# Routed experts: the second bias added by VectorE in fp32 at the copy out of PSUM, instead of by a product on TensorE

## The reference

```
h      = concat(patch embedding, n-gram text embedding)        # [64, 229, 128]
h      = h + attention(layernorm(h))
t      = layernorm(h)
shared = sum over 2 shared experts of gelu(t W1 + b1) W2 + b2
probs  = softmax(t gate_w + gate_b); the top 2 of 8 experts e per row, weight p
routed = sum over those 2 of p * (gelu(t rW1[e] + rb1[e]) rW2[e] + rb2[e])
out    = h + shared + routed
```

## Time and profile before

| | |
|---|---|
| runs | 1188.53, 1191.96, 1196.56 us |
| median | 1191.96 us |
| profiled execution | 1194.19 us |
| its span in the trace | 1192.5 us |
| granted TensorE clock, mean | 0.99 |
| busy share of the span | PE 96%, PEld 72%, DVE 80%, POOL 71%, ACT 66% |

### The profile page before, as it was taken

How to read it: one execution, slowest core, us unless ns; L and a number is a source line. 1 busy time by engine, 2 the same in 40 slices (tenths; PEclk the granted TensorE clock), 3 DMA queues, 4 the chain that set the end, 5 groups by cost and what they waited for, 6 DMA issues and landing times.

```text
span 1192.5 us, 31733 instructions
## 1 busy us (share of the span) xinstructions
PE 1142.3 (96%) x9318; PEld 860.6 (72%) x9318; DVE 950.8 (80%) x2484; ACT 791.6 (66%) x1835; POOL 842.8 (71%) x808
## 2 busy tenths in 40 slices
PE   7999999999999999889999989999999999999998
PEld 4777777777777778644545468998989999955555
DVE  5788898888888888879976756676767777779997
ACT  2566666666766666546554557777777777768886
POOL 4446877777778786667887857777777777776664
PEclk9999999999999999989999999999999999999999
DMA  7245555555655553433344234454554444449998
GB/s 218 64 138 144 158 149 158 154 159 150 170 156 155 165 141 99 124 102 104 108 114 122 83 63 101 96 94 92 91 95 93 98 95 98 88 89 208 201 199 167
DMA packets 242871, 152.10 MB, mean 128 GB/s; under 512 B 153852, under 2 KB 221561, under 8 KB 242708
## 3 DMA queue, kind: packets, MB, share of 16 engines
q1 hardware_dynamic: 201684, 102.21, 34.7%
q0 software_dynamic: 36992, 40.97, 16.0%
q10 hardware_dynamic: 4032, 6.88, 2.2%
HBM read 70.74 MB, written 56.32 MB: 107 GB/s over the span
## 4 chain that ended last, share of the span: by engine, by line
POOL 39%; issue 24%; PE 17%; SPq 7%; DVE 3%; DMA 3%; ACT 3%; POOLq 0%; ACTq 0%; DVEq 0%
POOL slots_dram L1620 9%; POOL slots_dram L507 9%; POOL y_dram L1631 6%; SPq L1561 4%; POOL rstd L548 3%; POOL rstd L554 3%; POOL emb L477 2%; POOL slots_dram L517 2%; SPq L1562 2%; PE bank L1919 2%; PE bank L1943 2%; POOL w_part_lo L497 2%; PE bank L1921 2%; PE bank L1920 2%; PE bank L1944 2%
## 5 line engine op out<-in xcount | busy, mean ns | idle before, releaser
L1631 POOL DMA_INDIRECT y_dram<-y_sb,y_row x244 | 267.3, 1095 | 96.5 <-issue 72.5
L1714 ACT ACTIVATE gel_all<-bank,b 128x256 f32<-128x256 f32 x488 | 191.8, 475 | 47.8 <-PE bank L1921 45.1
L1347 ACT ACTIVATE gel_all<-bank,b 128x458 f32<-128x458 f32 x256 | 154.8, 640 | 89.8 <-PE bank L1341 61.4
L1942 PE MATMUL bank<-w_part_hi,hid_all 128*128 x976 | 171.0, 219 | 0.0
L1833 DVE CAST hid_all<-gel_all 128x1024 f16<-128x1024 f32 x122 | 86.3, 708 | 105.1 <-ACT gel_all L1714 105.1
L1944 PE MATMUL bank<-w_part_hi,hid_all 128*128 x976 | 169.7, 219 | 0.0
L1943 PE MATMUL bank<-w_part_lo,hid_all 128*128 x976 | 169.7, 219 | 0.0
L507 POOL DMA_INDIRECT slots_dram<-row_bufs,slot_1st x128 | 133.9, 1046 | 46.2 <-issue 36.8
L1835 DVE TENSOR_TENSOR hid_all<-gel_all,hid_all 128x1024 f16<-128x1024 f32 x122 | 149.5, 1226 | 4.2
L1358 DVE TENSOR_TENSOR hid_all<-gel_all,hid_all 128x916 f16<-128x916 f32 x128 | 142.5, 1113 | 4.4
L1919 PE MATMUL bank<-xT_r,w_part_hi 128*128 128x256 f16 x488 | 134.0, 275 | 9.5 <-DMA tags_r<-slots_dram 8.4
(11 more groups left out here) (189 smaller groups left out, 2887.4 us busy)
## 6 DMA issues: line engine op xcount, KB each, us to landing
xin<-in_xmain SPq DMA_DIRECT2D x32, 771.8 KB
x2r_dram<-row_bufs SPq DMA_DIRECT2D x32, 260.0 KB, 2.3
x2t_dram<-x2T SPq DMA_DIRECT2D x32, 240.0 KB, 6.4
x_cols<-x2t_dram ACTq DMA_DIRECT2D x28, 240.0 KB, 3.0
row_bufs<-x2r_dram SPq DMA_DIRECT2D x24, 260.0 KB, 2.8
stage<-in_ffn_w SPq DMA_DIRECT2D x20, 256.0 KB, 5.6
xin<-in_xrest SPq DMA_DIRECT2D x32, 128.6 KB
y_dram<-y_sb,y_row POOLq DMA_INDIRECT x244
```

Of the source, the lines that this page charges most:

```text
L1347: act.activation(self.gel[:, f // 2 % 2, f % 2, :], self.up_dst(k, f), ACT.Gelu, bias=self.b1[:, f:f + 1]).then_inc(self.gel_ready, 1)
L1631: pool.indirect_dma_start(out=y_dram, in_=y_sb[:, s, c, :], in_offset=None, out_offset=bass.IndirectOffsetOnAxis(ap=y_row[:, s, c:c + 1], ...
L1714: act.activation(gel[:, s8 % 2, f, :], up_bank[s8 % 2][half][:, (f % 2) * TILE:(f % 2 + 1) * TILE], ACT.Gelu, bias=of_expert(b1, SHARED * ...
L1942: pe.matmul(part, h_hi, w2_hi, start=False, stop=False)
```

## The change

The routed second bias is no longer turned into halves in the attention stage: its memset, its two loads and the four POOL operations are gone, and so is the product that put it into the bank. Instead, the bias of all eight experts is loaded in fp32 for all partitions (128 x 1024 elements, 512 KB, from an input that already has 128 equal rows) by one DMA on SP into the first two of `row_bufs`, once these are free, among SP's waits ahead of the first tile load. DVE gets the expert number too (`Experts(dve)`) and a new instruction per tile, `add_bias`: it reads the bank and the bias row of the tile's expert and writes the sum to `y_sb`. It stands ahead of `split` in DVE's step, three tiles late. ACT scales `y_sb` in place, three tiles late instead of two. PE waits for the sum (`biased`) instead of the scaled result. In `down` the chunks are now the outer loop and the slices the inner one. The last tile is summed on DVE behind the second split of late pair 0 and scaled on ACT behind GELU 5 instead of 3.

The hunks that only pass `b2` and `routed_b2` through signatures are left out:

```diff
@@ -65,9 +65,7 @@
 TILE_CH = TILE // P
 TILES = (2 * TOKENS + EXPERTS * (TILE - 1)) // TILE
 WORDS = -(-TILES // 4)
-B2_LO = 32
-B2_COLS = EXPERTS * HID
-B2_STEPS = 5
+B2_STEPS = 1
 EARLY_PAIRS = 18
 LATE_PAIRS = PAIRS - EARLY_PAIRS
 LOGITS_AT, ROUTE_AT = PAIR_SEQ, PAIR_PATCHES
@@ -255,9 +252,6 @@
         wstage = stage[:, 0:WBLOCK].rearrange("p (s c) -> p s c", c=P)
         x_space = x_cols[:, :, :, :].bitcast(FP32).rearrange("p a h n -> p (a h n)")
         rows_again = [space[:, 0:4 * ROW].rearrange("p (c w) -> p c w", w=ROW) for space in (x_space, stage)]
-        b2_space = acc[:, NCH - 32:NCH, :].rearrange("p c d -> p (c d)")
-        b2_in = b2_space[:, 0:2 * B2_COLS].rearrange("p (h c) -> p h c", h=2)
-        b2_low = b2_space[:, 2 * B2_COLS:2 * B2_COLS + B2_COLS // 2].bitcast(FP16)
 
         route_cols = slice(ROUTE_AT, ROUTE_AT + (GROUP + 1) * EXPERTS)
         tokb_bank, tr1_bank, tr2_bank, o_bank = bank[0], bank[1], bank[2], bank[7]
@@ -306,7 +300,7 @@
         var2_ready, rstd2_ready, shift2_ready = sem("var2_ready"), sem("rstd2_ready"), sem("shift2_ready")
         ws_hi, ws_done, top_kept = sem("ws_hi"), sem("ws_done"), sem("top_kept")
 
-        b2_zeroed, b2_loaded, b2_up = sem("b2_zeroed"), sem("b2_loaded"), sem("b2_up")
+        b2_loaded, b2_up = sem("b2_loaded"), sem("b2_up")
         N_W = 10
         FIRST_BANKS, BANKS_UP = 3, 19
         WARM = 28
@@ -378,9 +372,6 @@
             for c, (at, n) in enumerate(CHUNKS):
                 sp.dma_start(rel[0:n, c, :], w_rel[at:at + n, :]).then_inc(w_in, 16)
             load_w(0)
-            sp.wait_ge(b2_zeroed, 1)
-            for n, row in enumerate((0, B2_LO)):
-                sp.dma_start(b2_in[row:row + 1, n, :], routed_b2[0:1, :]).then_inc(b2_loaded, 16)
             for s in range(SHARED):
                 sp.dma_start(shared_col[:, s:s + 1], shared_b2[0, s:s + 1, :].rearrange("o d -> d o")).then_inc(b2_loaded, 16)
             sp.dma_start(b1[:, :], ffn_b1).then_inc(w_late, 16)
@@ -458,7 +449,6 @@
                 for at in (region_at, next_at):
                     pool.iota(at[:, 4 * n:4 * n + 4], pattern=[[REGION, 4]], base=4 * n * REGION, channel_multiplier=0,
                               allow_small_or_imprecise_dtypes=True).then_inc(const_p, 1)
-            pool.memset(b2_space[:, 0:2 * B2_COLS], 0.0).then_inc(b2_zeroed, 1)
             pool.wait_ge(const_p, 14)
             pool.affine_select(out=until[:, :], in_=until[:, :], compare_op=ALU.is_ge, fill=0.0, base=0,
                                pattern=[[-1, P]], channel_multiplier=1).then_inc(tables, 1)
@@ -519,21 +509,10 @@
                     out_offset=bass.IndirectOffsetOnAxis(ap=slot_2nd[0:m, 4 * k + c:4 * k + c + 1], axis=0)
                 ).then_inc(again_out[k % 2], 16)
 
-            def sum_biases(n):
-
-                if n > 0:
-                    pool.wait_ge(b2_up, n)
-                if n == 0:
-                    pool.wait_ge(b2_loaded, 64)
-                    pool.tensor_tensor(shared_col[:, 0:1], shared_col[:, 0:1], shared_col[:, 1:2], ALU.add).then_inc(b2_up, 1)
-                elif n == 1:
-                    pool.tensor_copy(b2[:, :], b2_in[:, 0, :]).then_inc(b2_up, 1)
-                elif n == 2:
-                    pool.tensor_copy(b2_low[:, :], b2_in[:, 1, :]).then_inc(b2_up, 1)
-                elif n == 3:
-                    pool.tensor_tensor(b2_low[:, :], b2_in[:, 1, :], b2_low[:, :], ALU.subtract).then_inc(b2_up, 1)
-                elif n == 4:
-                    pool.tensor_tensor(b2[:, :], b2[:, :], b2_low[:, :], ALU.add).then_inc(b2_up, 1)
+            def sum_biases():
+
+                pool.wait_ge(b2_loaded, 32)
+                pool.tensor_tensor(shared_col[:, 0:1], shared_col[:, 0:1], shared_col[:, 1:2], ALU.add).then_inc(b2_up, 1)
 
             def keep_top(b):
 
@@ -577,8 +556,8 @@
                     front_powers(i + 3, 1 - p)
                 if last_ahead:
                     sum_text(j + 2)
-                if isinstance(i, int) and 2 <= i < 2 + B2_STEPS:
-                    sum_biases(i - 2)
+                if i == 2:
+                    sum_biases()
 
             def end_step(i, j, q):
 
@@ -1445,6 +1424,7 @@
         y = scratch[:, :].rearrange("p (b i c w) -> p b i c w", b=Y_BUFS, i=2, c=2)
 
         rows_s = row_bufs
+        b2_rows = row_bufs[:, 0:2, :, :].rearrange("p b c w -> p (b c w)")[:, 0:EXPERTS * HID]
         gel_s = gel_all[:, 0:4 * PAIR_SEQ].rearrange("p (j f n) -> p j f n", j=2, f=2)
         hid_s = hid_all[:, :].rearrange("p (s h f n) -> p s h f n", s=2, h=2, n=PAIR_SEQ)
         gel = gel_all[:, :].rearrange("p (s f n) -> p s f n", s=2, f=NF)
@@ -1470,6 +1450,7 @@
         up_done, down_done = sem("rup_done"), sem("rdown_done")
         gel_ready, hid_hi, hid_ready = sem("rgel_ready"), sem("rhid_hi"), sem("rhid_ready")
         y_ready, row_set = sem("y_ready"), sem("row_set")
+        b2_in, biased = sem("b2_in"), sem("biased")
         y_out = [sem(f"y_out{n}") for n in range(Y_TILES)]
         y_in = [sem(f"y_in{n}") for n in range(Y_BUFS)]
         summed = [sem(f"summed{n}") for n in range(Y_BUFS)]
@@ -1587,6 +1568,8 @@
             sp.wait_ge(fill_out, 16 * (EXPERTS + 1))
             for b in range(ROWS_BUFS):
                 sp.wait_ge(scattered[b], 64 * uses(b, ROWS_BUFS, PAIRS - AGAIN))
+                if b == 1:
+                    sp.dma_start(b2_rows, routed_b2).then_inc(b2_in, 16)
             sp.wait_ge(done.again_out[1], 64 * uses(1, 2, AGAIN))
             for t in range(TILES):
                 load_tile(t)
@@ -1698,12 +1681,9 @@
 
             def out_y(t, s8):
 
-                act.wait_ge(down_done, t + 1)
-                if reaches(t, Y_TILES):
-                    act.wait_ge(y_out[s8], 2 * TILE_CH * (t - s8))
+                act.wait_ge(biased, t + 1)
                 for c in range(TILE_CH):
-                    last = act.activation(y_sb[:, s8, c, :], down_bank[s8 % 2][:, c * HID:(c + 1) * HID], ACT.Copy,
-                                          scale=tags[:, s8, c, 1:2])
+                    last = act.activation(y_sb[:, s8, c, :], y_sb[:, s8, c, :], ACT.Copy, scale=tags[:, s8, c, 1:2])
                 last.then_inc(y_ready, 1)
 
             def gelu(t, s8, e, half):
@@ -1720,8 +1700,8 @@
                 e = experts.of(s8 % 4, NF)
                 gelu(t, s8, e, 0)
                 gelu(t, s8, e, 1)
-                if reaches(t, LAG):
-                    out_y(t - LAG, (s8 - LAG) % 8)
+                if reaches(t, LAG + 1):
+                    out_y(t - LAG - 1, (s8 - LAG - 1) % 8)
 
             experts = Experts(act)
             act.wait_ge(tables_up, 3)
@@ -1729,6 +1709,7 @@
             act.wait_ge(early.hid_ready, NJ * EARLY_PAIRS)
             tiles(act, step)
 
+            out_y(TILES - 3, (TILES - 3) % 8)
             out_y(TILES - 2, (TILES - 2) % 8)
             act.wait_ge(hid_ready, TILES)
 
@@ -1743,7 +1724,7 @@
             for k in range(LATE_PAIRS):
                 for f in range(NG):
                     late.gelu(act, k, f)
-                    if k == 0 and f == 3:
+                    if k == 0 and f == 5:
                         out_y(TILES - 1, (TILES - 1) % 8)
                     if f % 4 == 3:
                         for i in combined(k, f // 4):
@@ -1834,13 +1815,30 @@
                 dve.wait_ge(hid_hi, t + 1)
                 dve.tensor_tensor(hid[:, s, 1], gel[:, s8 % 2], hid[:, s, 0], ALU.subtract).then_inc(hid_ready, 1)
 
+            def add_bias(t):
+                if t == 0:
+                    dve.wait_ge(b2_in, 16)
+                if t % 4 == 0:
+                    experts.load(t // 4)
+                e = experts.of(t % 4, P)
+                dve.wait_ge(down_done, t + 1)
+                dve.tensor_tensor(y_sb[:, t % Y_TILES], down_bank[t % 2][:, 0:TILE_CH * HID].rearrange("p (c d) -> p c d", d=HID),
+                                  b2_rows[:, bass.ds(e, HID)].rearrange("p (c d) -> p c d", c=1).to_broadcast([P, TILE_CH, HID]),
+                                  ALU.add).then_inc(biased, 1)
+
             def step(t, s8, four):
+                if reaches(t, LAG + 1):
+                    add_bias(t - LAG - 1)
                 split(t, s8)
                 y_rows(t, s8)
                 if t == 0:
                     early.accumulate(dve, EARLY_PAIRS - 1)
 
+            experts = Experts(dve)
+            dve.wait_ge(tables_up, 3)
             tiles(dve, step)
+            add_bias(TILES - 3)
+            add_bias(TILES - 2)
 
             def add_y(i):
                 dve.wait_ge(scaled, i + 1)
@@ -1856,6 +1854,8 @@
                     if k == 1 and j == 0:
                         dve.wait_ge(down_done, TILES)
                     late.split(dve, k, k % 2, j)
+                    if k == 0 and j == 1:
+                        add_bias(TILES - 1)
                     if k > 1 and j == 1:
                         late.accumulate(dve, k - 2)
                     if j % 2 == 1:
@@ -1927,21 +1927,18 @@
```

(19 more changed lines are left out.)

17 lines of the change are left out of this document (8 added, 9 removed).

## The result

| | before | after |
|---|---|---|
| median of 20 runs each, alternating | 1193.87 us | 1197.40 us |
| ratio | | 1.0029, 95% interval 1.0016 to 1.0042 |
| profiled execution, span | 1192.5 us | 1194.7 us |

The time hardly moves, as forecast, but the sum had 0.0 and the measured difference is +3.5 us (2 to 5): the changed kernel is a little slower. A second measurement on another chip gave 1.0032 (1.0015 to 1.0050; 1194.41 to 1198.27 us). The 13.3 us of bias products are gone from TensorE and do not show in the end.

What follows compares the result with a forecast made beforehand. SP's loads at 2.83 us a tile were taken to pace PE; +0.5 (results later) - 0.5 (PE's slack there) = 0.0, so the median forecast was 1192.0 us, own range 1188 to 1196.

Steps and rivals of the forecast that it cites:

- rival C: Late tile counts in full: combining starts 2.8 us later, PE's slack gives back 0.5; +2.3, 1194.3 us; chance 0.18.
- SP sets the pace of the routed tiles: Routed tiles: SP's own speed is 2.83 us a tile, held by no semaphore; PE, needing 2.79, follows it.
- The 2.1 us of lead: End of routed tiles: PE is 6.67 - 4.6 = 2.1 us behind SP, all a faster PE can win there.
- My 4.6: Routed tiles: middle time in us from SP's load issue to PE's start when PE waits (4.1 to 5.1).
- PE's saving of 0.11 us a tile: Routed tiles: 122 bias products of 0.11 us removed, 13.3 us of PE, taking it from 2.79 to 2.68 a tile.
- the new order of the products: Routed tiles on PE: chunk outside, slice inside, same widths and same pairs of equal weights; cost 0.
- Rival A: The saving goes through as SP's pace drops towards 2.68 us a tile: 1178 to 1185, middle 1182; chance 0.14.
- The results one tile later, "+0.5 us": POOL and combining: results 2.79 us later, less 1.3 PE lead, 0.65 early gain, 0.3 ACT wait: about 0.5 later.
- The late pairs: ACT's wait for the first combined row grows from 2.61 to 6.2 us; only 0.5 of PE's 3.05 us kept.
- Attention, 0.65 us: Start-up and attention: a memset and four POOL instructions gone; PE's two steps shorten from 30.28 to 29.62, gaining 0.65 us.
- DVE, ACT: Routed tiles: DVE's sum of 0.42 us fits idle time, cost 0; ACT scaling from SBUF instead of PSUM, 0.
- rivals B and D: B: VectorE becomes the bound, 1204.5 us, chance 0.08. D: the sum blocks POOL's scatters, 1236 us, chance 0.02.

Runs made afterwards that it cites:

- the other trace with the product: Kernel before, with only the last tile's result scaled behind six of the late pair's activations in place of four: 1193.52 us, ratio 0.9995.
- packed pairs: Changed kernel with two row addresses a word (0.9930), against kernel before (0.9962) and kernel without the routed second bias (0.9881), both with the same packing.
- packed kernels: VectorE packs two tiles' row addresses in a word, so SP does one register load for two tiles: kernel before 1187.92 us, changed kernel 1184.03 us.
- the run with nothing but the delay: Kernel without the routed second bias, each scatter held until the next tile's result is ready, nothing added to VectorE: 1195.53 us, ratio 1.0011.
- the second trace: The changed kernel itself, unchanged, run again beside the kernel before on another chip: 1198.27 us, ratio 1.0032.
- packed addresses: Two tiles' row addresses in one 22-bit word, one SP register load for both; on the changed kernel 1184.03 us, ratio 0.9930.
- the packed kernel before: Kernel before with two row addresses a word, one SP register load and bound check for two tiles: 1187.92 us, ratio 0.9962.

## Why the prediction was right, and where it was not

*The number.* The forecast of 1192.0 us started from a median of 1191.96; the measured ratio of 1.0029 makes 1195.4 of that. It lies at the upper edge of the own range of 1188 to 1196, nearer to rival C's 1194.3 than to the forecast. That 13.3 us of removed work gain nothing was worked out and holds. That the rest of the sum came to 0.0 did not: it was +0.5 less 0.5, and both the lead and the later results in it were wrong in size. The range was wide enough to hold that.

*SP sets the pace of the routed tiles: right, and shown.* SP stayed at 2.83 to 2.9 us a tile with and without the product, and the only edit that opened the stage was one on SP: -4.5 us on the kernel before, -12 on the changed one. "A gain of 13.3 us on PE's account ends as none" stands, by the run that removes the product and adds no work (1.0020). PE's wait for tags grew from 5.0 to 9.1 us, less than the "far more" that was foretold, because about half of the 13.3 us was given back inside PE's steps (below).

*The 2.1 us of lead: mis-sized.* Measured 0.9 to 1.2 (6.7 in the trace before, 5.5 to 5.8 in four without the product), and nothing against the other trace with the product, where the lead is 5.0. My 4.6 was the middle of leads *with a wait* at early tiles; at the end the last tile still stood 5.5 to 5.8 us behind its load.

*PE's saving of 0.11 us a tile: mis-sized.* It is 0.05 to 0.07 once SP doesn't hold PE (339.2 us for the stage with the product, 333.0 and 331.2 without it), since the step behind a new word of expert numbers gives about half of it back. The prediction put the new order of the products at 0, because widths and weights are the same; it did not ask when PE's sequencer has the addresses. By the distances in `down` that term is some 6 us of PE's time, though no run has the order alone. I had found the word's load on ACT's sequencer and charged it to DVE, but not looked at it on PE's. Rival A's "13.3" was never there to have.

*The results one tile later, "+0.5 us": this is the step that failed.* I had the full tile, 2.79, and took 1.3 us of lead, 0.65 of attention and 0.3 of ACT's wait off it. Relative to PE's last tile nothing comes off the start of the combining: +3.2 and +3.5 us in the packed pairs, +1.5 and +3.2 in the changed kernel itself. Three errors made it: of the lead that I took off at most 0.9 was there; the distance grows by about a tile in mid-stage and by more at its end (in the packed kernels the scaled result follows PE's first product of its tile by 9.2 us before and 11.5 after, +2.3, and GpSimd starts 0.35 us later behind it; for the last tile it is 8.8 and 12.1, +3.3); and its backlog at the end did not hide this (its scatters stay a fixed distance behind the results). Rival C, "the late tile counts in full", had this mechanism (+2.8 less 0.5, 1194.3) and I gave it 0.18. What is shown is the later start of the combining; how much of it reaches the median time is open, as the run with nothing but the delay says.

*The late pairs: right in kind, too large.* ACT's wait for the first combined row was to grow from 2.6 to about 6 us and PE to idle some 2.5 us: measured 4.83 (3.06 in the second trace) and 2.07. The 6 us counted on a PE that arrives 3.05 us earlier; its last tile started 0.69 us earlier.

*Attention, 0.65 us: right.* The pair of steps that took 30.28 us takes 29.62 (123.79 to 153.41).

*DVE, ACT, and rivals B and D: right.* The sum takes 0.41 us for 0.42 (0.412 mean), casts still have idle time before them (0.39 us in the median), and PE's pace with the sum is that without it (2.74 and 2.75 us a tile, packed). ACT's scaling from SBUF takes 0.70 us for two, 0.63 from PSUM. Of 109 scatters beside a sum 97 take 0.98 us, the short time, and the scatters' mean over the stage went from 1087 to 1100 ns (1103 in the second trace). So the sum does not block GpSimd. By the rule of the Trainium skill, "SBUF — State Buffer", section "Who interferes with whom", a VectorE instruction with one SBUF input, outside the two-port modes, leaves the shared port alone; the trace agrees, with these 0.98 us.

*What stays open.* The terms that I can measure are -0.65 (attention), -0.9 to 0 (lead) and +1.5 to +3.2 (results), together 0 to +2.5 us; the measured +3.5 (2 to 5) is more. The run with all removals and no addition is at +2.4 us (-0.2 to +5) where these terms give -0.7 to -1.6, so it is 3 us above its terms (0.5 at the low end of the interval). Since this run adds nothing, what is missing seems to come with the removal or the new order of the loops, and not with the sum. SP's way of 343 to 350 us could hold them: a PE that waits for loads is exposed to each of SP's long issues. But that way differs as much between two executions of one kernel (345.4 and 349.8), and no run separates it.

## What to carry to other kernels

An engine at 99% busy may still follow another: compare the distance between starts on both, and see whether the feeder waits for a semaphore. If it does not, its own instructions (here a register load and a bound check for every tile) are the place to save, and only then is work taken off the fed engine worth anything. A result that is made one step later starts the stage that waits for the last one later by about that step (1.5 to 3.6 us here for a tile of 2.8), and time saved elsewhere must not be netted against it unless it lies on the same chain. And a new order of the same products is not free by itself: it sets how soon the engine's sequencer must have each address. Compare the distances between starts, step by step, before and after.

The best correct kernel of this study is the change together with the packed addresses, 0.9930 of before. It is so only where the kernel before takes 1194 us; at 1385 it was 1.5 to 1.7% slower, and the packed kernel before, 0.9962 and 0.9911, is the one that gained in both.

## What the runs showed of the hardware

- The same kernel takes 1193 to 1194 us on three of the chips of the experiments and 1385 on two, where distances of about 0.7 us (0.055 is usual) stand between PE's products with nothing that the profile shows being waited for. A change can be faster in one regime and slower in the other: 0.993 and 1.017.
- PE's narrow products can wait for the addresses of their weights. Address operations stood 0.11 to 0.12 us apart on PE's sequencer; with two of them for every 3 products of 0.055 us, PE's distances grew to 0.10 and 0.11 in the steps behind a register load, and 24 products took 1.52 us instead of 1.30.
- SP's issues alone can pace a stage: a transposing load (1.21 us), a tag copy (0.42), a register load and its check repeat every 2.66 us undisturbed and 2.83 to 2.90 on average, with no wait of SP in the profile. Without the register load two loads were 2.20 us apart.
- Scatters of 128 rows beside VectorE's sum out of PSUM take 0.98 us in 97 of 109 cases (the longest 1.68); the others of the same stage take 1.12 us in the median and 0.98 to 1.49 in all. GpSimd keeps a fixed distance behind the results with no wait shown (2.23 us over 100 tiles in the packed kernel before).
